# A two-layer block on one core: state-space layers with two power buffers, the kernel product behind the input product, a normalisation over eight PSUM banks, and a prologue in another order

## The reference

```python
def _layernorm_channels(z, w, b):          # over the 128 channels
    ...
def _s4d_layer(z, log_dt, A_re_log, A_im, C_re, C_im, D_skip, W, bvec):
    dt = jnp.exp(log_dt)
    A = -jnp.exp(A_re_log) + 1j * A_im      # 128 channels x 32 modes
    dtA = A * dt[:, None]
    C = (C_re + 1j * C_im) * (jnp.expm1(dtA) / A)
    K = 2.0 * jnp.einsum('hn,hnl->hl', C, jnp.exp(dtA[:, :, None] * l)).real
    y = causal convolution of z with K      # by FFT in the reference
    y = jax.nn.gelu(y + z * D_skip[:, None])
    out = jnp.einsum('oh,bhl->bol', W, y) + bvec[None, :, None]
    return out[:, :Hh] * jax.nn.sigmoid(out[:, Hh:])
for i in range(4):
    z = _layernorm_channels(h, ln_w[i], ln_b[i])
    h = _s4d_layer(z, ...) + h
```

## Time and profile before

| | us |
|---|---|
| median of 3 runs | 1367.76 |
| lowest, highest | 1367.61, 1373.05 |
| profiled execution | 1377.83 |
| its span, first to last instruction | 1376.0 |
| PE, DVE, ACT, POOL busy | 1062.0, 774.7, 531.4, 408.1 |
| mean granted TensorE clock | 0.843 |

### The profile page before, as it was taken

One profiled execution on the slowest core, in us unless ns is written; L12 is line 12 of the kernel. 1 busy time (PEld: TensorE's weight loads), 2 busy tenths in 40 slices (PEclk: granted clock), 3 DMA queues, 4 the chain that ended last, 5 costly groups with the idle time before them and its releaser, 6 DMA issues.

```text
span 1376.0 us, 20521 instructions
## 1 busy us (share of the span) xinstructions
PE 1062.0 (77%) x7980; PEld 711.6 (52%) x7980; DVE 774.7 (56%) x1365; ACT 531.4 (39%) x1254; POOL 408.1 (30%) x476
## 2 busy tenths in 40 slices
PE   5766784884745339999999867759789697979877
PEld 3444553562543227878787743335466443556633
DVE  1538456474473724546464579859755436945443
ACT  1266425517312513030302060026688134768622
POOL 0250601603400730000000034429744224944310
PEclk9975865966866559999999989979899688979868
DMA  3034405306132457272723030000112200012100
GB/s 88 1 68 71 95 2 97 66 2 120 43 55 41 184 108 126 57 134 55 129 61 73 27 121 0 0 0 1 31 33 73 78 1 26 1 32 64 32 0 31
DMA packets 60452, 76.60 MB, mean 56 GB/s; under 512 B 37464, under 2 KB 41956, under 8 KB 58596
## 3 DMA queue, kind: packets, MB, share of 16 engines
q1 hardware_dynamic: 60360, 75.36, 24.8%
HBM read 52.87 MB, written 1.51 MB: 40 GB/s over the span
## 4 chain that ended last, share of the span: by engine, by line
PE 52%; DVE 14%; POOL 12%; ACT 8%; issue 6%; SPq 4%; DMA 4%; DVEq 0%; POOLq 0%; ACTq 0%
PE psum L1131 6%; PE psum L1133 6%; PE psum L1132 6%; POOL rest L1361 3%; ACT rest L1314 3%; POOL rest L1351 3%; DVE main L489 3%; PE psum L1549 2%; POOL rest L1357 2%; PE psum L644 2%; SPq L954 2%; PE psum L572 2%; SPq L960 2%; PE psum L1558 2%; PE psum L1616 2%
## 5 line engine op out<-in xcount | busy, mean ns | idle before, releaser
L402 POOL TENSOR_TENSOR kept<-kept 128x8 f32<-128x8 f32 x12 | 2.4, 202 | 462.4 <-DVE kept L379 462.4
L1314 ACT ACTIVATE rest<-psum,main 128x128 f32<-128x128 f32 x256 | 113.4, 480 | 12.4 <-POOL main L1372 10.8
L978 ACT ACTIVATE x_high<-main 128x512 fp32r<-128x512 f32 x48 | 30.4, 633 | 199.2 <-DVE main L1052 199.2
L1131 PE MATMUL psum<-x_high,w_low 128*128 128x512 f32 x192 | 76.9, 400 | 20.1 <-DVE x_low L1057 20.1
L676 PE MATMUL psum<-main 128*32 128x64 f32 x1024 | 23.6, 279 | 76.1 <-DMA main<-main 76.0
L415 ACT ACTIVATE main<-psum,kept 128x128 f32<-128x128 f32 x40 | 14.5, 472 | 171.5 <-POOL kept L408 171.5
L1380 POOL TENSOR_TENSOR rest<-rest,main 128x512 f32<-128x512 f32 x64 | 65.4, 1043 | 47.1 <-DVE main L1445 47.1
L1131 PE MATMUL psum<-hid_high,w_low 128*128 128x512 f32 x192 | 75.6, 394 | 0.7 <-DVE main L1076 0.7
L1132 PE MATMUL psum<-x_low,w_high 128*128 128x512 f32 x192 | 76.1, 397 | 0.0
L1133 PE MATMUL psum<-x_high,w_high 128*128 128x512 f32 x192 | 76.1, 396 | 0.0
L1132 PE MATMUL psum<-hid_low,w_high 128*128 128x512 f32 x192 | 74.8, 389 | 0.0
(11 more groups left out here) (307 smaller groups left out, 2831.6 us busy)
## 6 DMA issues: line engine op xcount, KB each, us to landing
rest<-share_d SPq DMA_DIRECT2D x4, 3072.0 KB, 20.9
rest<-share_d SPq DMA_DIRECT2D x4, 2304.0 KB, 20.1
main<-main SPq DMA_DIRECT2D x32, 256.0 KB, 5.1
main<-k_pad SPq DMA_DIRECT2D x16, 512.0 KB, 7.4
rest<-main SPq DMA_DIRECT2D x32, 256.0 KB, 3.7
main<-w_dram SPq DMA_DIRECT2D x2, 3072.0 KB, 14.1
main<-main SPq DMA_DIRECT2D x32, 128.0 KB, 4.3
rest<-tables_dram SPq DMA_DIRECT2D x2, 2048.0 KB, 9.2
```

Source lines behind the costliest of these rows:

```text
L1131: T.matmul(dst, w_small, x_large, start=first, stop=False)
L1314: last = A.activation(probs[:, p, 4 * r + m, :], bank[2 * p + r][:, m * P:(m + 1) * P], ACT.Exp, scale=row_scale[:, c, r, m:m + 1], bias=r ...
```

## The change

- **Buffers.** `pow_re` and `pow_im` exist twice, by the layer's parity. `k_rows` now lies in `yT`. `skip` of all four layers is loaded once, in the prologue. The power sines wait only for the move of two layers earlier.
- **Order on PE in a layer.** Near angles 0 and 1 (banks 4, 5) before the input product; near angles 2 and 3 behind it; then K with its skip column in one bank (63 columns a product and one column, bank 0, behind DVE's transposes); then far angles; then exponents, behind the rows' copy.
- **Projection.** Gate and gated matmul are apart: one gate bank (5), two gated banks (4, 6). Between the blocks stand turned-back groups. Four groups go ahead of the projection (`EARLY`), not six.
- **Normalisation.** Only behind all four projection blocks. Centring uses banks 0, 2, 5, 0 and scores 7, 4, 2, 6. DVE writes full-height blocks to `z_rows` (new, in `b_im` and `s_a`), four operations a block; moves to `zu` are done by POOL (lower half of blocks 0, 1), DVE (lower half of 2, 3) and ACT (upper halves).
- **DVE in a layer.** The inverse stands at the start of the layer, near turns behind the turned input, far turns behind the scans and ahead of u; the wait for POOL's phases stands behind far turns.
- **POOL.** The ten first operations of the coefficients are a function of their own (`s4_pool_residues`) ahead of the decay. All reciprocal roots and POOL's two moves stand between the fourth and the fifth phase operation.
- **SP.** `expo` before `wmod`; `ln_wb` of the next layer is loaded once z is ready, ahead of the convolution rows.
- **Prologue.** PE starts with the angles; modulation products between near and far angles; tokens behind the far angles; powers ahead of the normalisation on DVE; sines ahead of the layer norm on ACT; turned-back groups and normalisation interleaved as in a layer.

```diff
-        pow_re = keep(HG, CHUNK)
-        pow_im = keep(HG, CHUNK)
+        pow_re = [keep(HG, CHUNK) for _ in range(2)]
+        pow_im = [keep(HG, CHUNK) for _ in range(2)]
...
-        CENTRED, SCORED, TURNED_BACK = 0, 2, (1, 3)
+        CENTRED, SCORED, TURNED_BACK = (0, 2, 5, 0), (7, 4, 2, 6), (1, 3)
+        GATED, GATE, KERNEL, RATES = (4, 6), 5, 0, 0
-        EARLY = 6
+        EARLY = 4
...
+        def s4_dve_norm(dve, N):
+
+            s4_dve_eps(dve, N, 0)
+            s4_dve_eps(dve, N, 1)
+            s4_dve_z_rows(dve, N, 0)
+            s4_dve_eps(dve, N, 2)
+            s4_dve_z_rows(dve, N, 1)
+            s4_dve_eps(dve, N, 3)
+            s4_dve_z_rows(dve, N, 2)
+            s4_dve_z_rows(dve, N, 3)
+            for b in (2, 3):
+                s4_dve_z(dve, N, b)
...
+        def s4_pe_norm(pe, N, back):
+
+            s4_pe_centre(pe, N, 0)
+            s4_pe_centre(pe, N, 1)
+            s4_pe_back(pe, N, range(back, back + 2))
+            s4_pe_var(pe, N, 0)
+            s4_pe_var(pe, N, 1)
+            s4_pe_centre(pe, N, 2)
+            s4_pe_z(pe, N, 0)
...
             if more:
-                s4_pe_near_angles(pe, L + 1)
+                pe.wait_ge(sem("s4_dtaT"), L + 2)
+                pe.wait_ge(sem("s4_z_rows"), L * 6 + 2)
+                s4_pe_near_angles(pe, L + 1, (0, 1))
             pe.wait_ge(sem("s4_back"), (L + 1) * BACKS)
-            pe.wait_ge(sem("s4_z"), (L + 1) * BLOCKS)
+            for name, n in (("s4_z_rows", 6), ("s4_z_pool", 2), ("s4_z_act", 4)):
+                pe.wait_ge(sem(name), (L + 1) * n)
...
+        def s4_pool_norm(pool, N):
+
+            for b in range(BLOCKS):
+                s4_pool_rstd(pool, N, b)
+            for b in range(2):
+                pool.wait_ge(sem("s4_z_rows"), N * 6 + b + 1)
+                nc.gpsimd.tensor_copy(*z_half(b, 0)).then_inc(sem("s4_z_pool"), 1)
```

More of the change, by code:

```diff
@@ L601, in s4_pe_centre @@
                 pe.wait_ge(sem("s4_h"), (N - 1) * BLOCKS + b + 1)
-            if b:
-                pe.wait_ge(sem("s4_var_eps"), N * BLOCKS + b)
-            nc.tensor.matmul(bank[CENTRED][:, :], centre, hT[:, 512 * b:512 * b + 512], start=True, stop=True).then_inc(sem("s4_centred"), 1)
+            if b == 2 and N:
+                pe.wait_ge(sem("s4_sig"), N * BLOCKS)
+            if b == 3:
+                pe.wait_ge(sem("s4_var_eps"), N * BLOCKS + 1)
+            nc.tensor.matmul(bank[CENTRED[b]][:, :], centre, hT[:, 512 * b:512 * b + 512], start=True, stop=True).then_inc(sem("s4_centred"), 1)
         def s4_pe_var(pe, N, b):
@@ L609, in s4_pe_var @@
             for t in range(4):
-                last = nc.tensor.matmul(bank[CENTRED][:, t:t + 1], h_sq[b % 2][:, t * P:(t + 1) * P], mean_col, start=True, stop=True)
+                last = nc.tensor.matmul(bank[CENTRED[b]][:, t:t + 1], h_sq[b % 2][:, t * P:(t + 1) * P], mean_col, start=True, stop=True)
             last.then_inc(sem("s4_var"), 1)
         def s4_pe_z(pe, N, b):
-            if b:
-                pe.wait_ge(sem("s4_z"), N * BLOCKS + b)
-            else:
+            if b == 0:
@@ L618, in s4_pe_z @@
                 pe.wait_ge(sem("s4_weighted"), N + 1)
+            if b == 2:
+                pe.wait_ge(sem("s4_var_eps"), N * BLOCKS + 2)
+            if N and b in (1, 3):
+                pe.wait_ge(sem("s4_h"), (N - 1) * BLOCKS + (3 if b == 1 else 4))
             for t in range(4):
                 c = 4 * b + t
-                last = nc.tensor.matmul(bank[SCORED][:, t * P:(t + 1) * P], hT[:, c * P:(c + 1) * P], weighted, start=True, stop=True)
+                last = nc.tensor.matmul(bank[SCORED[b]][:, t * P:(t + 1) * P], hT[:, c * P:(c + 1) * P], weighted, start=True, stop=True)
@@ L622, in s4_pe_z @@
             last.then_inc(sem("s4_z_ps"), 1)
+        def s4_pe_norm(pe, N, back):
[6 more added lines that the diff above has]
+            s4_pe_z(pe, N, 0)
+            s4_pe_back(pe, N, range(back + 2, back + 3))
+            s4_pe_centre(pe, N, 3)
+            s4_pe_z(pe, N, 1)
+            s4_pe_var(pe, N, 2)
+            s4_pe_z(pe, N, 2)
+            s4_pe_back(pe, N, range(back + 3, back + 5))
+            s4_pe_var(pe, N, 3)
+            s4_pe_z(pe, N, 3)
+            s4_pe_back(pe, N, range(back + 5, BACKS))
@@ L624, in s4_pe_glu @@
         def s4_pe_glu(pe, L, b):
+            rhs = yT[:, 512 * b:512 * b + 512]
+            if b:
+                pe.wait_ge(sem("s4_sig"), L * BLOCKS + b)
+            nc.tensor.matmul(bank[GATE][:, :], w_out[:, P:2 * P], rhs, start=True, stop=True).then_inc(sem("s4_gate_ps"), 1)
             if b >= 2:
                 pe.wait_ge(sem("s4_h"), L * BLOCKS + b - 1)
-            rhs = yT[:, 512 * b:512 * b + 512]
-            for k in range(2):
-                last = nc.tensor.matmul(bank[4 + 2 * (b % 2) + k][:, :], w_out[:, k * P:(k + 1) * P], rhs, start=True, stop=True)
@@ L631, in s4_pe_glu @@
[L631 removed]
+            nc.tensor.matmul(bank[GATED[b % 2]][:, :], w_out[:, 0:P], rhs, start=True, stop=True).then_inc(sem("s4_glu_ps"), 1)
         def s4_pe_layer(pe, L, more):
             T = nc.tensor
[L635 to L636 removed]
             if more:
[L638 removed]
+                pe.wait_ge(sem("s4_dtaT"), L + 2)
+                pe.wait_ge(sem("s4_z_rows"), L * 6 + 2)
+                s4_pe_near_angles(pe, L + 1, (0, 1))
@@ L945, in s4_sp_layer @@
                 sp.dma_start(dst, dram[name][L]).then_inc(sem("s4_glu_in"), 16)
-            sp.wait_ge(sem("s4_k_rows"), rows)
+            if L + 1 < S4_LAYERS:
+                sp.wait_ge(sem("s4_z_rows"), one * 6)
+                sp.dma_start(ln_wb, dram["ln_wb"][L + 1]).then_inc(sem("s4_ln_in"), 16)
+            sp.wait_ge(sem("s4_k_rows"), one)
             for q in range(PIECES):
@@ L1711, in _ @@
             s4_pool_weighted(pool, 0)
-            for b in range(BLOCKS):
-                s4_pool_rstd(pool, 0, b)
             s4_pool_coefficients(pool, chain, 0)
-            s4_pool_phases(pool, chain, 0, lambda b: None)
+            s4_pool_phases(pool, chain, 0, lambda: s4_pool_norm(pool, 0))
             for L in range(S4_LAYERS - 1):
```

308 lines of the change are left out of this document (149 added, 159 removed).

## The result

| | before | changed |
|---|---|---|
| median, us | 1370.37 (4 runs) | 1319.81 (4 runs) |
| lowest, highest | 1367.61, 1373.05 | 1315.53, 1323.25 |
| profiled execution, its span | 1377.83, 1376.0 | 1323.25, 1321.5 |
| mean granted TensorE clock | 0.843 | 0.848 |
| input products start at (profile) | 99.9, 195.1, 289.8, 381.9 | 71.3, 156.9, 241.9, 327.6 |

Changed to before: 0.963, 95% interval 0.9591 to 0.9669. The forecast was 1316 us. In the two profiles the whole difference of 54.5 us is there when the fourth input product starts (54.4).

A forecast was written before the change was run, and what follows sets the result against it. Four blocks handed back and forth through one score bank, then TensorE's slow near angles, set the end of the stretch between layers. Prologue 19.9, transitions 31.2 and end 0.7 sum to 51.8 us: 1367.8 to 1316 us, own range 1300 to 1336.

The forecast's parts named there:

- Prologue: Start up to the first input product: reached at 80.0 us instead of 99.9, 19.9 us saved, bounds 25.5 and 10.7.
- I take the turn at about 60 to 68: Prologue: moment, in us, at which TensorE's durations go from slow to full clock; before the change about 70.
- Transitions: Three stretches from the gelu's transpose to the next input product: 10.9, 12.0 and 8.3 us gained, together 31.2.
- the collision: Transitions' end: DVE's copies held by POOL's last two phase operations, charged 2.0 us a place, bounds 0 and 4.4.
- DVE gets in between the two: Transitions' end: DVE's copies run between POOL's last two phase operations of 2.35 us each, hence a 2.0 us charge.
- From the input to the output product: Stretch in each layer from input product to L676, 43 us: no change, plus or minus 1 us.
- wait ahead of u: DVE's far turns ahead of u, cover 3.5 us before SP asks; as rival, three layers by 3 us, 1325 us, 10%.
- Moves: Normalisation: POOL's new moves 1.0 us each, DVE's 512-column copies some 0.45, up to 0.75 with strided output.
- End: Last layer: the sigmoid starts one matmul earlier and the gated matmul ends the wait, 0.7 us saved.
- No collision: Rival: DVE's copies run beside POOL, 2 us at four places, 1308 us, 17%.
- Half the gain: Rival: hand-overs between engines, POOL's moves or strided copies cost more; 26 us gained, 1342 us, 12%.
- the half clock throughout: Rival: TensorE at half clock through projection and normalisation, 8.5 to 9.6 us lost per transition, 1383 us, 3%.

The follow-up runs named there:

- Experiments 5: Changed kernel with the prologue's near and far sines on ScalarE behind the first layer norm, as before the change: 1319.06 us, first input product at 79.4 us.
- experiment 6: Changed kernel with all four score products through one bank, each block waiting until DVE has read the one before: 1323.54 us.
- experiment 1: Changed kernel with POOL's last two phase operations waiting until DVE's two copies are through: 1292.26 us, ratio to before 0.944.
- experiment 3: Changed kernel with one pair of power buffers instead of two, the sines waiting for the move of the layer before: 1311.29 us.
- experiment 4: Changed kernel with DVE writing z at half height straight to its place, without the eight moves, the eight banks kept: 1321.82 us.
- experiment 8: Changed kernel plus one 1.76 us DVE memset in the last block of the fourth layer's projection: 1313.05 us, ratio 0.9588.
- experiment 11: Changed kernel plus two DVE memsets in a row in the last block of the fourth layer's projection: 1315.92 us (1312.37 to 1320.9).

## Why the prediction was right, and where it was not

The total: 51.8 us forecast, 50.6 measured between the medians, 54.5 between the profiles. Two terms were wrong and cancelled: the prologue gave 8.7 us more, the transitions 5.4 less. That the total came so close was luck; the direction and the places of the gain were not.

- **Prologue: 19.9 forecast, 28.6 measured, outside its bounds (10.7 to 25.5).** The step that failed is the moment at which the clock turns. "I take the turn at about 60 to 68": it came at about 50. From powers to input product I had 30.9 us and 24 at full clock; it took 25.2. The powers were also 3.0 us earlier than reckoned (46.1 for 49.1), 1.6 us of it as the near angles started at 11.8, not 13.4. Experiments 5 and 6 show two parts of the gain: without early sines 8.1 us are lost, without the score banks 10.5. They don't have to add up, and what the other reorderings of the prologue are worth was not tested.
- **Transitions: 31.2 forecast (10.9, 12.0, 8.3), 25.8 measured** (periods of 85.6, 85.0 and 85.7 instead of 95.3, 94.7 and 92.1: 9.7, 9.7, 6.4). The mis-sized term is the collision. It was the right mechanism at the right place, weighed at 2.0 us with bounds 0 and 4.4, both too low. The wait was that of both phase operations and a bit of a move: the pair took 6.3 us instead of 1.2, so 5.1. "DVE gets in between the two" was an assumption from a single row where POOL had only one operation. The rest of the sum ran 1.7 us early. 3.1 more lost and 1.7 won, three times, are 4.2 of the 5.4 us that are missing. Another 1.8 us lie in the stretch of the next point.
- **From the input to the output product: plus or minus 1.** It took 44.1, 43.5 and 44.4 us against 43.5, 43.1 and 43.7 before: within the bound, but 0.4 to 0.8 us longer each time. The new wait ahead of u had 3.7 us of cover where I had 3.5: u_re is there at 185.85, SP asks at 189.56.

```profile
184.66 1.19 DVE L564 TENSOR_TENSOR rest<-main 128x992 f32<-128x992 f32 x1
```

```profile
189.56 7.03 SPq L1016 DMA_DIRECT2D main<-rest  x8
```

- **Moves.** POOL's took 1.07 us each (1.0 taken), DVE's free 0.58 (0.45 taken, 0.75 allowed for strides), full-height rows 0.34 (0.44). ScalarE's took 1.08 where I had let copies of 0.53 stand for them; it was hidden, and became the end of the chain only in experiment 1.
- **End: 0.7 forecast, 0.2 measured**, below what can be told.
- **Rivals.** "No collision" did not come; made so in experiment 1, it is worth more than the 8 us I gave it (18.1 up to the fourth input product), for the collision was larger and at one place TensorE's pause cost clock as well. "Half the gain", the wait ahead of u and the half clock throughout did not come. What no case of mine had is that TensorE's clock in untouched stages can move the time by 11 us. It did not disturb the comparison of the profiles: both had 994 us there. The executions behind the two medians have no trace to tell. Had the change happened to draw the other variant, as experiment 3 did, the result would have read some 1310 us.

## What to carry to other kernels

Before putting two engines on copies at the end of a chain, look what stands next on GpSimd: a DVE copy between SBUF tiles can be held through all of its operations that follow back to back, and one wait put on GpSimd (or the copies on DVE alone) is cheap. When an edit's total and its place in the trace disagree, believe the place: mark a few points of the chain and compare those, for the stages behind may run at another clock without having been touched (981 to 994 us here). And spread work over banks first where a stall would also lose TensorE's clock: one score bank cost 10.5 us in the prologue and 1.7, 0.4 and -0.3 us in the transitions.

## What the runs showed that I had not expected

- DVE lost against two consecutive POOL operations: 5.87 us for a copy of 0.58. An operation of DVE on PSUM with one SBUF tensor ran at 0.44 us beside the same operations (experiment 4).
- The untouched part behind the fourth input product took 981.2 to 994.1 us in eleven other kernels and the two compared. It parts where TensorE's clock comes back or doesn't. With a start 0.9 us later it took 9.8 us less between the profiles (experiment 8); which variant an execution gets can differ within one kernel (1312 to 1321 us in experiment 11). What decides it was not settled: I had two values in mind, and 987.5 and 991.5 came as well.
- A pause of TensorE can cost more than its length: three waits of together 6.7 us cost 10.5 (experiment 6). Ahead of the input product, taking a pause of 3.9 us away gave part of that product its full clock at one place of four; at the others it stayed at half clock (experiment 1).
- Windows in the prologue show a granted clock of 1.00 from the start, while one centring took 2.05 us at 50.7 us before the change, twice its duration at the full clock. There the durations must be believed, not the clock's row.
